# Mixing on two halves of TensorE's rows instead of one block-diagonal product

## What is computed

```python
agg_w = jnp.einsum('bk,koi->boi', att, weight[..., 0])
agg_b = att @ bias_k
y = jnp.einsum('boi,bih->boh', agg_w, x) + agg_b[:, :, None]
base = jnp.einsum('bsd,od->bso', y, base_W)
logits = jnp.einsum('bsd,ed->bse', y, router_W)
mid = jnp.einsum('bsd,edr->bser', y, lora_A) * w_dense[..., None]
out = x + base + jnp.einsum('bser,erd->bsd', mid, lora_B) * 2
```

## Time and profile before

| | |
|---|---|
| median of 3 runs | 962.93 us |
| the profiled execution's own time | 962.68 us |
| its span, first to last instruction | 960.9 us |
| PE busy with multiplies | 951.2 us |
| PE busy with weight loads | 878.3 us |
| DVE, ACT, POOL busy | 743.2, 236.9, 294.4 us |

### The profile page before, as it was taken

The page is one execution under the profiler, slowest core; times in us unless marked ns, Lnnn a source line. Parts: engine busy times, 40 slices in busy tenths (PEclk is TensorE's granted clock), DMA queues, the critical chain, the costliest instruction groups (busy, mean ns, idle before and its releaser), DMA issues.

```text
span 960.9 us, 17804 instructions
## 1 busy us (share of the span) xinstructions
PE 951.2 (99%) x5765; PEld 878.3 (91%) x5765; DVE 743.2 (77%) x1641; ACT 236.9 (25%) x541; POOL 294.4 (31%) x228
## 2 busy tenths in 40 slices
PE   8999999999999999999999999999999999999997
PEld 6998999999999999999999999999999999999996
DVE  5877877877777877778777778777778777788774
ACT  5444212222222222222222122222122222222210
POOL 3002333133332133332233331333321333322331
PEclk9999999999999999999999999999999999999999
DMA  8666234333334332344242343332343323443311
GB/s 350 184 200 181 72 115 139 112 113 104 103 115 136 108 116 91 103 128 129 96 130 76 115 136 113 111 108 99 115 136 110 113 96 107 119 135 93 132 46 44
DMA packets 46694, 116.04 MB, mean 121 GB/s; under 512 B 20433, under 2 KB 20561, under 8 KB 45521
## 3 DMA queue, kind: packets, MB, share of 16 engines
q1 hardware_dynamic: 45824, 111.54, 35.2%
q0 software_dynamic: 576, 4.19, 2.1%
q10 hardware_dynamic: 272, 0.03, 0.0%
HBM read 77.97 MB, written 33.59 MB: 116 GB/s over the span
## 4 chain that ended last, share of the span: by engine, by line
PE 98%; DVE 1%; ACT 0%; issue 0%; POOL 0%; POOLq 0%; DVEq 0%; ACTq 0%
PE pc L499 17%; PE pa L510 13%; PE pb L510 13%; PE y_ps L471 12%; PE pb L513 9%; PE pa L513 9%; PE pd L499 9%; PE pd L554 4%; PE pc L554 4%; PE pc L536 1%; PE pd L536 1%; PE pa L524 1%; PE pb L524 1%; PE pd L544 1%; PE pa L527 1%; PE pb L527 1%
## 5 line engine op out<-in xcount | busy, mean ns | idle before, releaser
L471 PE MATMUL y_ps<-mix_w,x_sb 128*128 128x128 f32 x1024 | 193.9, 274 | 0.0
L394 POOL TENSOR_TENSOR out_sb<-out_sb,u 128x512 f32<-128x512 f32 x90 | 127.8, 1450 | 202.2 <-DVE u L1109 202.2
L471 PEld LDWEIGHTS y_ps<-mix_w,x_sb 128*128 128x128 f32 x1024 | 167.9, 190 | 12.3 <-issue 0.5
L364 POOL TENSOR_TENSOR ya<-ya 128x512 f32<-128x512 f32 x30 | 39.9, 1331 | 380.0 <-DVE ya L1014 380.0
L1014 DVE TENSOR_TENSOR ya<-y_ps,bias_sb 128x512 f32<-128x512 f32 x128 | 87.8, 687 | 37.5 <-PE y_ps L471 33.8
L499 PE MATMUL pc<-w_hi,s_hi 128*128 128x512 f32 x240 | 99.1, 413 | 0.0
L510 PE MATMUL pa<-w_hi,a_hi 128*128 128x376 f32 x240 | 94.6, 394 | 0.7 <-ACT p L825 0.7
L499 PE MATMUL pc<-w_hi,s_lo 128*128 128x512 f32 x240 | 94.4, 393 | 0.0
L499 PE MATMUL pc<-w_lo,s_hi 128*128 128x512 f32 x240 | 93.8, 391 | 0.0
L817 ACT ACTIVATE mid_hi<-pd 128x128 fp32r<-128x128 f32 x62 | 17.2, 278 | 273.2 <-PE pd L544 273.2
L810 ACT ACTIVATE exps<-logits,neg_max 128x8 f32<-128x8 f32 x64 | 19.3, 301 | 264.5 <-DVE neg_max L1031 264.5
(11 more groups left out here) (214 smaller groups left out, 2553.7 us busy)
## 6 DMA issues: line engine op xcount, KB each, us to landing
x_sb<-in_x SPq DMA_DIRECT2D x64, 512.0 KB, 3.8
out_sb<-in_x SPq DMA_DIRECT2D x64, 512.0 KB, 4.4
out<-out_sb SPq DMA_DIRECT2D x64, 512.0 KB, 2.8
w_raw<-in_base_t SPq DMA_DIRECT2D x5, 1024.0 KB, 11.3
w_raw<-neg POOLq DMA_DIRECT2D x4, 1024.0 KB, 10.4
bias_sb<-bias_rows SPq DMA_DIRECT2D x62, 64.0 KB, 4.8
w_raw<-in_side SPq DMA_DIRECT2D x1, 544.0 KB, 6.8
lb_raw<-in_lora_b SPq DMA_DIRECT2D x1, 512.0 KB, 14.1
```

The lines of the kernel that those rows point to most:

```text
L364: nc.gpsimd.tensor_tensor(y_block(0, 1), y_block(0, 1), y_block(0, 0), ALU.subtract).then_inc(s3_set, 1)
L394: nc.gpsimd.tensor_tensor(o, o, u2[:, :], ALU.add).then_inc(done, 1)
L471: mm = nc.tensor.matmul(y_ps[q % 2][:, j * P:(j + 1) * P], x_sb[m][:, c * P:(c + 1) * P], mix_w[m][:, :], start=True, stop=True)
```

## The change

A tile's two batches are no longer b and b + 1 of a block-diagonal matrix; they take rows 0 to 63 and 64 to 127 of PE, 64 rows each, as two products. Each loads its own 64 rows of the chunk of x (128 columns) and multiplies its batch's own 64 x 64 matrix; the results go to different PSUM banks, `y_ps[0]` and `y_ps[1]`. So a bank holds one batch of each tile instead of one tile. No zeros are multiplied, and neither `summed`, `place_mix` nor the zeroing is there: DVE's sum writes `mix_w[k][m]`, two sets of it in turn.

The mixing of a pair is no longer spliced between chunks. It is done in two stretches of 32 products, 8 chunks each: `mix(p + 1, 0, ...)` after P1 and `mix(p + 1, 1, ...)` after P7. There are two counts of `mixed` to a pair instead of four. DVE adds the bias after each stretch in two instructions, one for each bank. In DVE's and ACT's order `split_low` and `split_high` of A11 come earlier, and the second stretch's bias adds stand ahead of the sum u.

x is loaded in four DMAs of 256 KB a pair, after one wait for the mixing of the pair before; the bias of a pair comes in one DMA after a wait for y. The batches of a tile are two apart instead of one, and the start-up tables that pick batches (`pick_half`, `parity4`, `own_tile`) follow, with one more small sum.

```diff
-                c = h * HALF + j
-                mm = nc.tensor.matmul(y_ps[q % 2][:, j * P:(j + 1) * P], x_sb[m][:, c * P:(c + 1) * P],
-                                      mix_w[m][:, :], start=True, stop=True)
-                if j == HALF - 1:
-                    mm.then_inc(mixed, 1)
+            def mix(n, h, k):
+                if not (first(n) and h == 0):
+                    pe.wait_ge(y_ready, 4 * n + 2 * h)
+                for m in range(2):
+                    if h == 0:
+                        pe.wait_ge(x_in[m], 32 * n + 32)
+                        pe.wait_ge(summed_set, 2 * n + m + 1)
+                    for j in range(HALF):
+                        c = h * HALF + j
+                        for b in range(PAR):
+                            rows = slice(b * C, (b + 1) * C)
+                            to = y_ps[b][:, :].rearrange("p (s j m r) -> p s j m r", s=2, j=HALF, m=2)
+                            mm = nc.tensor.matmul(to[:, :, j, m, :], x_sb[m][rows, c * P:(c + 1) * P],
+                                                  mix_w[k][m][rows, :].rearrange("i (s r) -> i s r", s=2),
+                                                  start=True, stop=True)
+                mm.then_inc(mixed, 1)
...
             def body(p, k):
...
                     mm = product_with_side(A11, B11, pa, j, 0, True)
                     if j == HALF - 1:
                         mm.then_inc(p1_mm, 1)
-                    mixed_in(0, j)
...
+                if not last(p):
+                    mix(p + 1, 0, 1 - k)
...
                     mm = product_with_side(S3, T3, pb, j, 0, True)
-                    if j == HALF - 1:
-                        mm.then_inc(p7_mm, 1)
-                    mixed_in(2, j)
+                mm.then_inc(p7_mm, 1)
+                if not last(p):
+                    mix(p + 1, 1, 1 - k)
...
-            def place_mix(n, m):
...
-                nc.vector.tensor_reduce(summed[m][:, :], of[:, :].rearrange("p (c k) -> p c k", k=K), AX.X,
+                nc.vector.tensor_reduce(mix_w[k][m][:, :], of[:, :].rearrange("p (c k) -> p c k", k=K), AX.X,
...
+                for b in range(PAR):
+                    nc.vector.tensor_tensor(to[:, :, :, b, :],
+                                            y_ps[b][:, :].rearrange("p (s j r) -> p s j r", s=2, j=HALF),
+                                            bias[:, :, b, :].unsqueeze(2).broadcast_to([P, 2, HALF, C]),
+                                            ALU.add).then_inc(y_ready, 1)
...
+            def load_x(n):
+                sp.wait_ge(mixed, 2 * n)
+                for m in range(2):
+                    read_x(n, m)
+                sp.wait_ge(y_ready, 4 * n)
+                sp.dma_start(bias_sb[:, :].rearrange("p (s r) -> p s r", s=2),
+                             bias_dram.rearrange("s (p r) -> p s r", p=NP)[n, :, :].partition_broadcast(P)
+                             ).then_inc(bias_in, 16)
```

More of the change, by code:

```diff
@@ L93, in adaln_ffn_kernel @@
         u2_at, u2 = place("u2", BANK)
-        mix_w = [place(f"mix_w{m}", P)[1] for m in range(2)]
-        bias_sb = [place(f"bias_sb{m}", P)[1] for m in range(2)]
+        mix_w = [[place(f"mix_w{k}{m}", C)[1] for m in range(2)] for k in range(2)]
+        _, bias_sb = place("bias_sb", 2 * PAR * C)
         _, ident = place("ident", P)
@@ L115, in adaln_ffn_kernel @@
         _, att_rows = place("att_rows", NT * K)
-        summed = [place(f"summed{m}", C)[1] for m in range(2)]
         assert top[0] <= 229344
@@ L187, in adaln_ffn_kernel @@
         x_in = [sem(f"x_in{m}") for m in range(2)]
-        bias_in = [sem(f"bias_in{m}") for m in range(2)]
+        bias_in = sem("bias_in")
         res_in = [[sem(f"res_in{k}{s}") for s in range(2)] for k in range(2)]
@@ L299, in _ @@
             sp.wait_ge(bias_out, 16)
-            for m in range(2):
-                load_x(1, m)
+            load_x(1)
             load_residual(0, 0)
-            for m in range(2):
-                load_x(2, m)
+            load_x(2)
             load_residual(1, 1)
@@ L311, in body @@
                 if mixes_after(p):
-                    for m in range(2):
-                        load_x(p + 2, m)
+                    load_x(p + 2)
             def store(p, k):
@@ L459, in _ @@
             keep_warm(2)
[L461 to L469, removed]
-                c = h * HALF + j
-                mm = nc.tensor.matmul(y_ps[q % 2][:, j * P:(j + 1) * P], x_sb[m][:, c * P:(c + 1) * P],
-                                      mix_w[m][:, :], start=True, stop=True)
-                if j == HALF - 1:
-                    mm.then_inc(mixed, 1)
[L476 to L482, removed]
+            def mix(n, h, k):
[14 more added lines that the diff above has]
+                mm.then_inc(mixed, 1)
+            mix(0, 0, 0)
+            pe.wait_ge(spread_set, 1)
+            nc.tensor.matmul(pb[:, BANK:], parity[:, :], att_spread[:, :], start=True, stop=True
+                             ).then_inc(att_rows_mm, 1)
+            mix(0, 1, 0)
             SPLITS = ((op_hi, w_hi), (op_hi, w_lo), (op_lo, w_hi))
@@ L625, in plain_pair @@
                 up(1, pc, False, plain_up)
-                for j in range(HALF):
-                    mix_chunk(p + 1, 3, j)
                 for j in range(HALF):
@@ L786, in _ @@
                           bias_rows[:, :].rearrange("b (s c) -> b s c", s=2)).then_inc(bias_out, 16)
-            place_mix(0, 0)
             act.wait_ge(bias_bc_mm, 1)
[L789 to L793, removed]
+            nc.scalar.copy(bias_sb[:, :].rearrange("p (s b c) -> p b s c", s=2, b=2 * PAR),
+                           bias_bc.rearrange("p (b s c) -> p b s c", s=2, b=2 * PAR)).then_inc(bias_set, 1)
             act.wait_ge(side_in, 16)
@@ L851, in first_pair @@
                     take_hi(B22, n)
-                for m in range(2):
-                    place_mix(1, m)
                 negate(B22, 1, neg_b22_set)
@@ L864, in first_pair @@
                 split_high(A12, 1, y_ready, 8)
-                for m in range(2):
-                    place_mix(2, m)
                 split_high(A22, 1, y_ready, 8)
@@ L883, in second_pair @@
                 split_high(S3, 2, s3_set, 1)
-                for m in range(2):
-                    place_mix(3, m)
                 split_mid(3, plain_up, 6, pc)
@@ L904, in body @@
                         take_hi(T4, n)
+                if not last(p):
+                    split_high(A11, p + 1, y_ready, 4 * p + 6)
                 exponents(2 * p)
                 if not last(p):
-                    split_high(A11, p + 1, y_ready, 4 * p + 6)
                     split_high(S3, p + 1, s3_set, p)
@@ L937, in scale_mix, with sum_mix @@
                                         ALU.mult).then_inc(scaled_set, 1)
-            def sum_mix(n, m, of):
+            def sum_mix(n, m, of, k):
                 dve.wait_ge(scaled_set, 2 * n + m + 1)
-                if not first(n):
-                    dve.wait_ge(mix_set[m], PAR * n)
-                nc.vector.tensor_reduce(summed[m][:, :], of[:, :].rearrange("p (c k) -> p c k", k=K), AX.X,
+                if not (isinstance(n, int) and n < 2):
+                    dve.wait_ge(mixed, 2 * n - 2)
+                nc.vector.tensor_reduce(mix_w[k][m][:, :], of[:, :].rearrange("p (c k) -> p c k", k=K), AX.X,
                                         ALU.add).then_inc(summed_set, 1)
@@ L949, in _ @@
                                   ident[:, 0:2 * PAR].unsqueeze(2).broadcast_to([P, 2 * PAR, P])).then_inc(hot_set, 1)
[L950 to L955, removed]
+            nc.vector.tensor_copy(pick_half[:, :].rearrange("j (m b p) -> j m b p", m=2, b=PAR),
+                                  ident[:, 0:2 * PAR].rearrange("j (b m) -> j m b", m=2).unsqueeze(3).broadcast_to(
+                                      [P, 2, PAR, C])).then_inc(pick_set, 1)
+            nc.vector.tensor_copy(pick_row[:, :].rearrange("j (b p) -> j b p", b=2 * PAR),
+                                  ident[:, 0:2 * PAR].unsqueeze(2).broadcast_to([P, 2 * PAR, P])
+                                  ).then_inc(pick_set, 1)
+            nc.vector.tensor_reduce(parity4[:, :], ident[:, :].rearrange("j (p b) -> j b p", p=NP), AX.X, ALU.add
                                     ).then_inc(pick_set, 1)
-            nc.vector.tensor_reduce(own_tile[:, :], by_tile, AX.X, ALU.add).then_inc(pick_set, 1)
+            nc.vector.tensor_reduce(own_tile[:, :].rearrange("j (p m) -> j p m", m=2),
+                                    ident[:, :].rearrange("j (p b m) -> j p m b", b=PAR, m=2), AX.X, ALU.add
+                                    ).then_inc(pick_set, 1)
             dve.wait_ge(pick_set, 3)
+            nc.vector.tensor_reduce(parity2[:, :], parity4[:, :].rearrange("j (b m) -> j b m", m=2), AX.X, ALU.add
+                                    ).then_inc(pick_set, 1)
+            dve.wait_ge(pick_set, 5)
             nc.vector.tensor_copy(parity[:, :].rearrange("j (b i) -> j b i", b=PAR),
```

(16 more changed lines are left out.)

90 lines of the change are left out of this document (26 added, 64 removed).

## The result

The changed kernel takes 989.4 us (median of 4 runs, 989.3 to 991.9) against 963.05 us: a ratio of 1.028, interval 1.0262 to 1.0298. The profiled execution's span grew from 960.9 to 987.5 us, by 26.6 us; 983 us had been forecast, 957 to 1100 as the range.

A forecast was written before the change was run, and what follows sets the result against it. PE's queue was taken to bound the kernel. Loads side by side 0, switches +20 and the rest 0, on the profiled execution's 962.7 us, made 983 us; range 957 to 1100.

The forecast's parts named there:

- The bound: Whole kernel: PE's queue, busy 99% of the span, sets the time; other engines count only if PE waits for them.
- What sets the pace: In mixing, the load sets the 0.112 us step, so halving the columns multiplied gains nothing by itself.
- Side by side: In mixing, loads of the two row halves run beside each other, so doubled loads add 0; with paid switches, 40%.
- The switches: At both ends of 64 mixing stretches, 128 changes of array shape at 0.16 us each: +20 us.
- 1098 us: Rival for mixing: both halves' loads queue for one path, four loads a chunk, +115 us plus 20 for shape changes; 22%.
- mixing would at best have halved: Rival for mixing: a chunk costs 0.112 us, -57 us, with shape changes 926 us in all; 8%.
- the 0.9 us wait for w_lo: At the start, PE's existing wait was said to cover the first pair's changes of array shape.
- clock rival: Rival: the clock falls to 1.2 GHz in 62 mixing stretches of 1.8 us, giving 1095 us or beyond; 4%.
- The edits costed at nothing: On ACT, POOL, DVE and SP: fewer copies and memsets, regrouped bias adds, new DMAs and waits; 0 us in all.
- free switches: Rival at the mixing stretches: halves load beside each other and shape changes cost nothing; 957 to 963, about 960 us; 14%.
- its step of 0.109 us: In mixing, a step a group of 16 would give if its last multiply lasted 0.333 us; saves 4 us.
- The floor: For mixing, the change at best costs today's price, only if the halves' loads run wholly beside each other.

The follow-up runs named there:

- one half after the other: Changed kernel with each stretch reordered: all 8 chunks on one half of the rows, then all 8 on the other; 1129.8 us.
- wide multiplies there: Kernel taking all chunks of one row half before the other's, with mixing multiplies of 128 columns in place of 64; 1090.3 us.
- the warm start: Changed kernel plus four more full-size 512-column keep-warm multiplies between the first and second tile of the very first stretch; 989.7 us.
- The wide multiplies: Changed kernel with each of its 2048 mixing multiplies taking 128 columns instead of 64; 990.8 us.
- adding switches: Changed kernel with each stretch cut in two (1008.9 us) or in four (1048.9 us), adding changes of the array's shape.
- all rows in two stretches: Kernel before, block-diagonal products on all 128 rows kept, but mixing grouped after P1 and after P7; 960.9 us, in more rounds 961.5.
- the start mended: Changed kernel with the first pair's x loaded ahead of the side columns and its first tile's mixing multiplied with 128 columns; 983.1 us.

## Why the prediction was right

**The bound.** PE's queue was the time, before and after. Where all the terms were foreseen, a sum over PE's items gave the time to within 1 or 2 us. It missed where a term was not: the clock with one half after the other (1104 forecast, 1129.8 measured), the start with wide multiplies there (12 us), and the warm start, which gained nothing of 3 to 6 us.

**What sets the pace.** The load, as the equal steps for 8, 64 and 128 columns in the earlier trace rows said. The wide multiplies show it directly: twice the columns, 1.99 against 1.93 us. That was the mechanism of the prediction, and it was right.

**Side by side.** This was the choice between cases that no row of before could make, and it decided between 983 and 1098 us. The trace of the changed kernel answers it (32 loads in 1.86 us), and so does turning the order (3.32 us). By the rule of the Trainium skill, "TensorEngine Tiling (Array Packing)" (Theoretical Speedup), up to 2x, mixing would at best have halved; the row of 1.86 us, against 1.88 for the sixteen loads on all rows, shows none of it. Here each half loads its own 128 columns of x, so the loads have doubled.

**The switches.** 0.16 us was taken, from one row at the low level, which allowed anything from 0.12 to 0.25; measured were 0.17 in two traces side by side, and 0.168 and 0.171 by adding switches. That the choice came within 0.01 us is in part luck. 62 stretches after the first pair's two make 62 x 0.34 = 21 us, where 20 had been forecast for all. Grouping, which the sum left out, gave back 1 to 2.

**What was missed: the start.** The prediction said that the 0.9 us wait for w_lo covers the first pair's switches, and costed the rest of the start at nothing. Its clock rival thought of stretches in the middle of the kernel. There the clock held (granted 1.00), but at the start it was still low. Before the change it rose during the first mixing, at about 15 us by the steps of the earlier trace rows; now it rose at about 29 us. That and the wait for x, now the landing of two DMAs a tile, made 7 us. The account of the whole is 21 for the switches, less 1 to 2 for grouping, plus 7: 26 to 27 us, where 20 had been forecast.

**The edits costed at nothing** were nothing after the start. DVE's sum u is waited for once, 0.5 us, and ACT's 128 copies fewer bought no time. The 0.4 us for `out_sb` stand in the run with all rows in two stretches too, so they come with the order. At the start the new loads of x were not: they are the wait of 1.8 us.

**The lower bound.** The range went down to 957 us for free switches. The prediction's own working gives 962.7 - 4 = 959, and its step of 0.109 us comes out as (1.95 - 0.333) / 15 = 0.108. Neither touches the forecast of 983.

**The floor.** The best that this design could have done was the price of mixing before. So, by this sum, no mending of switches or start makes it win: the start mended gives 983 us, and the kernel with all rows in the same order 961.

## What to carry to other kernels

Ask first whether the load or the multiply sets the step of a small product, by comparing steps of rows whose multiplies differ in width. If it is the load, and the stationary operand keeps its width, splitting the contraction rows doubles the loads, and running them beside each other only wins back what was doubled. Count the changes of the array's shape and price them (0.17 us each here); group products of one shape, and interleave the two halves in the queue one by one.

## What had not been expected of the hardware

With the two halves taken in turn, 32 loads lie in 1.86 us, about one each 0.054 us; on one half they follow at a step of 0.11 us. Order in the queue decides: with one half after the other a stretch takes 3.32 us instead of 1.93.

Thirty-two multiplies of 64 columns on one half at a time, in an engine that is busy without a gap, were followed by a granted clock of 0.53, once a pair; with 128 columns in the same slots no stretch was (0.999 in the mean). With the two halves side by side 64 columns held it at 1.00. A busy PE in the profile is thus no sign that the clock will stay.

At the start four full-size multiplies of 512 columns, 2 us long, did not bring the clock up before the same large product; 128 columns in sixteen mixing multiplies of each stretch did, with the halves in turn. With one half after the other, 128 columns in all 32 did not: the full clock came at about 39 us. Why the one and not the others stays open: no run varied their place.
